# Layer-norm row factors spread through DRAM by DMA instead of by matmul, with weight-set loads moved to ScalarE's queue

## What is computed

```python
h = einsum('bct,bcd->bdt', x, cond_w[subjects])
q, k, v, g = h @ Wq, h @ Wk, h @ Wv, silu(h @ Wg)
beta = sigmoid(h @ Wb + bb)
q = layernorm(silu(causal_dwconv(q, qconv_w, qconv_b)).reshape(Bs, Ls, H, DK), qn_w, qn_b)
k = layernorm(silu(causal_dwconv(k, kconv_w, kconv_b)).reshape(Bs, Ls, H, DK), kn_w, kn_b)
# layernorm: (x - m) * rsqrt(var + eps) * w + b over the 128 of a head
S = (1 - b) * S + b * v[..., :, None] * k[..., None, :];  o = einsum('bhvk,bhk->bhv', S, q)
x = x + (o * g) @ Wo
hd = x @ W.T + ((x @ A.T) @ B.T) * s
x = x + ternary_ffn(hd)          # rms norm, rows quantised to int8, weights -1, 0, 1
```

## Time and profile before

| what | value |
|---|---|
| median of 3 runs | 2684.84 us |
| profiled execution | 2685.08 us |
| its span, first to last instruction | 2683.5 us |
| TensorE busy, matmuls | 95% |
| VectorE, ScalarE, GpSimd busy | 63%, 45%, 26% |
| mean granted clock of TensorE | 0.986 of 2.4 GHz |
| DMA queue of SyncE | 413.63 MB, 48.6% of the 16 engines' span |

### The profile page before, as it was taken

One profiled execution on the slowest core, in us unless ns is written; L12 is line 12 of the kernel. 1 busy time (PEld: TensorE's weight loads), 2 busy tenths in 40 slices (PEclk: granted clock), 3 DMA queues, 4 the chain that ended last, 5 costly groups with the idle time before them and its releaser, 6 DMA issues.

```text
span 2683.5 us, 39968 instructions
## 1 busy us (share of the span) xinstructions
PE 2556.3 (95%) x14536; PEld 1985.0 (74%) x14536; DVE 1688.5 (63%) x2848; ACT 1197.7 (45%) x1878; POOL 696.3 (26%) x764
## 2 busy tenths in 40 slices
PE   5889999999999999999999999999999999999996
PEld 4667777777777777777777777777777777777774
DVE  3766666666666666666656666666666666666653
ACT  3555544544444444354444444353444544444431
POOL 3465522212222212222212222222212212222220
PEclk8999999999999999999999999999999999999998
DMA  6775745445444555355354454444544445444540
GB/s 167 249 224 185 240 154 159 139 155 177 121 142 147 165 166 157 109 172 194 113 173 132 144 177 154 151 139 138 163 148 156 140 149 179 120 146 142 171 132 16
DMA packets 264554, 416.17 MB, mean 155 GB/s; under 512 B 102058, under 2 KB 126634, under 8 KB 264362
## 3 DMA queue, kind: packets, MB, share of 16 engines
q1 hardware_dynamic: 264362, 413.63, 48.6%
HBM read 360.86 MB, written 52.69 MB: 154 GB/s over the span
## 4 chain that ended last, share of the span: by engine, by line
PE 88%; DVE 4%; ACT 3%; issue 2%; SPq 1%; POOL 1%; DMA 0%; ACTq 0%; DVEq 0%; POOLq 0%
PE ring L1048 31%; PE pj_a L1048 26%; PE pj_b L1048 13%; PE ring L1264 4%; PE m L1254 3%; PE var L1222 2%; PE cen_q L1243 2%; PE cen_k L1243 1%; PE cen_k L1244 1%; PE cen_q L1244 1%; PE ring L1149 1%; PE ring L1066 1%; ACT hb L912 1%; PE var L1233 1%; PE m L1264 1%
## 5 line engine op out<-in xcount | busy, mean ns | idle before, releaser
L780 DVE SCALAR_TENSOR_TENSOR y_q<-pj_a,conv,y_q 128x504 f32<-128x504 f32 (+2 forms) x384 | 281.7, 734 | 360.2 <-ACT y_q L963 351.0
L498 POOL TENSOR_TENSOR og_lo<-gt,og_hi 128x512 fp32r<-128x512 f32 x128 | 165.1, 1290 | 922.3 <-ACT og_hi L993 922.3
L1048 PE MATMUL pj_a<-ht_hi,wg 128*128 128x512 f32 x1024 | 352.9, 405 | 2.2 <-DVE y_q L780 2.1
L1048 PE MATMUL pj_a<-ht_hi,wq 128*128 128x512 f32 x1024 | 345.0, 398 | 2.5 <-DVE ht_lo L626 1.5
L1048 PE MATMUL pj_b<-ht_hi,wk 128*128 128x512 f32 x1024 | 335.9, 389 | 0.0
L1048 PE MATMUL ring<-wo,og_hi 128*128 128x512 f32 x1024 | 321.5, 395 | 14.8 <-DVE acc L660 11.8
L1048 PE MATMUL ring<-wv,ht_hi 128*128 128x512 f32 x1024 | 320.8, 394 | 6.8 <-ACT hb L914 6.8
L780 DVE SCALAR_TENSOR_TENSOR y_k<-pj_b,conv,y_k 128x504 f32<-128x504 f32 (+2 forms) x384 | 281.8, 734 | 62.3 <-ACT y_k L963 53.2
L951 ACT ACTIVATE sq_q<-cen_q 128x512 f32<-128x512 f32 x128 | 76.7, 599 | 435.7 <-PE cen_q L1244 435.7
L1048 PEld LDWEIGHTS ring<-wo,og_hi 128*128 128x128 f32 x1024 | 190.4, 189 | 74.2 <-DVE acc L660 18.5
L1048 PEld LDWEIGHTS ring<-wv,ht_hi 128*128 128x128 f32 x1024 | 189.2, 188 | 74.0 <-issue 26.8
(11 more groups left out here) (202 smaller groups left out, 5084.4 us busy)
## 6 DMA issues: line engine op xcount, KB each, us to landing
wq<-parts_q SPq DMA_DIRECT2D x112, 512.0 KB, 4.1
wk<-parts_k SPq DMA_DIRECT2D x112, 512.0 KB, 4.5
wg<-parts_g SPq DMA_DIRECT2D x112, 512.0 KB, 3.7
wv<-parts_v SPq DMA_DIRECT2D x112, 512.0 KB, 6.4
wo<-parts_o SPq DMA_DIRECT2D x112, 512.0 KB, 6.1
keep<-keep_rows SPq DMA_DIRECT2D x256, 64.0 KB, 3.9
wo<-parts_w SPq DMA_DIRECT2D x28, 512.0 KB, 5.6
acc<-in_x_dram SPq DMA_DIRECT2D x8, 1024.0 KB, 5.5
```

The source lines that it names most:

```text
L498: G.tensor_tensor(og_lo[:, u % OG_RING, :], gt[:, u % GT_RING, :], og_hi[:, u % OG_RING, :].bitcast(F32), ALU.subtract).then_inc(S["oglo"], 1)
L780: V.scalar_tensor_tensor(out=yy[:, :, k:], in0=pp[:, :, :L - k], scalar=conv[:, i, h, 3 - k:4 - k], in1=yy[:, :, k:], op0=ALU.mult, op1=AL ...
L1048: last = T.matmul(psum, a, b, start=start and n == 0 and m == 0, stop=stop and n == len(pairs) - 1 and m == 2)
```

## The change

- `spread`, `rstd_hi`, `split_rstd`, the matrix `pick` and what made it are gone. SyncE writes the four rows of `rstd` (partitions 0, 32, 64, 96; 8 KB) to `r_rows` in DRAM, waits for that, and loads each row with a broadcast to all 128 partitions (256 KB each) into the buffers of `sq_q` and `sq_k`, whose squares are used up. `normalise` reads these.
- So `squares` waits for the product of the unit two before, and `seed` waits until the rows of the pair before were written out.
- `variance` stands between the projections of q and k, `seed` before the first tap of k, `newton` between the taps of q and k.
- The loads of whole sets and of x are issued by ScalarE at the start of a slot. The first o quarter of a group is loaded in slot 9 (was 8), the second in 11 (was 10), x in 13 (was 12).
- The first o quarter is made in slot 10 in place of 9, the third set of v from slot 9 in place of 10. The ring of gated heads has 7 places in place of 6.

```diff
-    9: ([("o", 0, 0, 0), ("f", -1, None, 0), ("quant", -1, None, 2), ("quant", -1, None, 3), ("o", 0, 0, 1)],
-        [("o", 0, 0, 2), ("f", -1, None, 1), ("o", 0, 0, 3)]),
-    10: ([("v", 0, 2, 0), ("xqt", -1, None, 2)], [("v", 0, 2, 1), ("xqt", -1, None, 3)]),
+    9: ([("v", 0, 2, 0), ("f", -1, None, 0), ("quant", -1, None, 2), ("quant", -1, None, 3)],
+        [("v", 0, 2, 1), ("f", -1, None, 1)]),
+    10: ([("o", 0, 0, 0), ("xqt", -1, None, 2), ("o", 0, 0, 1)], [("o", 0, 0, 2), ("xqt", -1, None, 3), ("o", 0, 0, 3)]),
...
+            def load_rstd(m):
+                sp.wait_ge(S["rr"], m + 1)
+                for j in range(4 if m else 0):
+                    sp.wait_ge(S[f"r_in_{'qk'[j % 2]}{j // 2}"], 16 * m)
+                sp.dma_start(r_rows, rstd[0:P:32, :]).then_inc(S["r_out"], 16)
+                sp.wait_ge(S["r_out"], 16 * (m + 1))
+                for j in range(4):
+                    x_ = "qk"[j % 2]
+                    sp.dma_start(sq[x_][:, j // 2, :], r_rows[j:j + 1, :].broadcast_to([P, GROUP])).then_inc(S[f"r_in_{x_}{j // 2}"], 16)
...
+                if U % 2 == 0 and 2 <= U <= UNITS:
+                    load_rstd(U // 2 - 1)
                 if H <= U + 1 < UNITS:
                     load_head("g", U + 1)
...
             def normalise(u):
                 for x_ in "qk":
-                    dve.wait_ge(S[f"bc_{x_}"], u + 1)
+                    dve.wait_ge(S[f"r_in_{x_}{u % 2}"], 16 * (u // 2 + 1))
                     dve.wait_ge(S[f"cc_{x_}"], u + 1)
                     c = c_[x_][:, u % C_RING, :]
-                    V.tensor_tensor(c, c, bc_banks[u % 2][x_][:], ALU.mult).then_inc(S[f"n_{x_}"], 1)
+                    V.tensor_tensor(c, c, sq[x_][:, u % 2, :], ALU.mult).then_inc(S[f"n_{x_}"], 1)
...
             def squares(x_, u):
                 act.wait_ge(S[f"cen_{x_}"], u + 1)
                 if u > 1:
-                    act.wait_ge(S["var"], u // 2)
+                    act.wait_ge(S[f"n_{x_}"], u - 1)
...
                 if m:
-                    act.wait_ge(S["r_split"], m)
+                    act.wait_ge(S["r_out"], 16 * m)
...
+            def load_sets(U):
+
+                g, h = divmod(U, H)
+                for part in range(SET):
+                    if g < GROUPS and h in (0, 4, 8, 12) and g * SETS + h // 4 >= SETS:
+                        load_v(g * SETS + h // 4, part)
+                    if h == (1 if g == GROUPS else 2) and g > 1:
+                        load_o(g * SETS - 1, part)
+                    if h == 5 and 1 <= g < GROUPS:
+                        load_w2(g - 1, part)
+                    if h == 9 and 1 <= g < GROUPS:
+                        load_o(g * SETS, part)
+                    if h in (11, 14) and 1 <= g < GROUPS:
+                        load_o(g * SETS + (1 if h == 11 else 2), part)
...
             for U in range(SLOTS):
                 if U < UNITS:
                     project("q", U)
-                    project("k", U)
                 if U % 2 == 0 and 2 <= U <= UNITS:
                     variance(U // 2 - 1)
-                if U % 2 and 0 <= U - 2 < UNITS:
-                    spread(U - 2)
+                if U < UNITS:
+                    project("k", U)
```

More of the change, by code:

```diff
@@ L135, in adaln_attn_ffn @@
         rstd = sb("rstd", [P, GROUP])
-        r_parts = sb("r_parts", [P, GROUP], F32R)
         keep = sb("keep", [P, 2, HALF])
@@ L447, in _ @@
                     sp.dma_start(bias_b, ffn_b.rearrange("(o d) -> o d", o=1).broadcast_to([P, D])).then_inc(S["rows_in"], 16)
-                if h == 8 and 1 <= g < GROUPS:
-                    for part in range(SET):
-                        load_o(g * SETS, part)
+                if U % 2 == 0 and 2 <= U <= UNITS:
+                    load_rstd(U // 2 - 1)
                 if H <= U + 1 < UNITS:
@@ L560, in _ @@
                     step(V.tensor_copy(ident_in[half, t, :], ident[half, half]))
-            step(V.tensor_tensor(signs[:], by32[:, :, 1:2], by32[:, :, 0:1], ALU.subtract))
-            step(V.tensor_reduce(is_low[:], by32[:, :, 1], AX.X, ALU.add))
-            step(V.tensor_scalar(ones, ident[:], 0.0, 1.0, ALU.mult, ALU.add))
-            for j in range(4):
-                step(V.tensor_scalar(pick[:, j, :], ones, signs[:, j, :], 0.0, ALU.mult, ALU.add))
             dve.wait_ge(S["wb_in"], 16)
@@ L831, in _ @@
                     taps("q", U)
+                if U % 2 == 0 and 2 <= U <= UNITS:
+                    newton(U // 2 - 1)
+                if U < UNITS:
                     taps("k", U)
@@ L837, in _ @@
                 take(U, 0)
-                if U % 2 == 0 and 2 <= U <= UNITS:
-                    newton(U // 2 - 1)
                 if 0 <= U - 3 < UNITS:
@@ L843, in _ @@
                     silu_lo("k", U)
-                if U % 2 == 0 and 2 <= U <= UNITS:
-                    split_rstd(U // 2 - 1)
                 take(U, 1)
@@ new lines, in load_o, with load_last_w2 @@
+            def load_o(s, part):
+                if part == 0:
+                    if s % SETS:
+                        act.wait_ge(*made("o", s - 1, HT - 1))
+                    else:
+                        act.wait_ge(*made("h", s // SETS - 1, HT - 1))
+                n = (s % SETS) * SET + part
+                act.dma_start(block_both("o", n), parts["o"][n]).then_inc(S["wo_in"], 16)
+            def load_last_w2(part):
+                if part == 0:
+                    act.wait_ge(*made("v", GROUPS * SETS - 1, HT - 1))
+                act.dma_start(block_both("v", part), parts_w2[part]).then_inc(S["wv_in"], 16)
@@ new lines, in load_w2 @@
+            def load_w2(g, part):
+                if part == 0:
+                    act.wait_ge(*made("o", SETS * g + SETS - 1, HT - 1))
+                    if g == 0:
+                        act.wait_ge(S["saved_o"], 16 * H)
+                        act.wait_ge(S["w2_out"], 64)
+                act.dma_start(block_both("o", part), parts_w2[part]).then_inc(S["wo_in"], 16)
+            def load_sets(U):
[11 more added lines that the diff above has]
+                        load_o(g * SETS + (1 if h == 11 else 2), part)
+                    if U == UNITS:
+                        load_last_w2(part)
+                if h == 13 and g + 1 < GROUPS:
+                    load_x(g + 1)
@@ L1011, in _ @@
                     gated_hi(U - 4)
+                if U % 2 == 0 and 2 <= U <= UNITS:
+                    seed(U // 2 - 1)
                 if U < UNITS:
@@ L1018, in _ @@
                     silu("q", U)
-                if U % 2 == 0 and 2 <= U <= UNITS:
-                    seed(U // 2 - 1)
                 take(U, 0)
```

107 lines of the change are left out of this document (22 added, 85 removed).

## The result

| | before | after |
|---|---|---|
| median of five runs each, us | 2684.84 | 2698.37 (2693.86 to 2701.81) |
| ratio, 95% interval | | 1.0048 [1.0034, 1.0063]: 0.5% slower |
| profiled execution, its span, us | 2685.1, 2683.5 | 2693.9, 2692.1 |
| first group (slots 0 to 15), us | 307.3 | 342.3 |
| groups 1 to 6, mean, us | 322.8 | 318.6 |

What follows compares the result with a forecast made beforehand. TensorE, 95% of the span, was taken as the bound: 2685.1 - 58.4 (`spread` matmuls) - 23.3 (`r_parts` wait) + 8 (exchanged tiles) + 7 (x) + 21 (first group) = 2639.4, stated as 2640 us; range 2606 to 2676.

Steps and rivals of the forecast that it cites:

- The matmuls' price: TensorE: removing the 256 `spread` matmuls, 0.228 us of the stream each, saves 58.4 us.
- The wait for `r_parts`: TensorE's wait before `spread`, 23.3 us in 11 places, was taken to go whole.
- C: Rival, 8%: issues on ScalarE cost twice SyncE's, so TensorE waits before variance in slots 2 and 14; 2660 us.
- D: Rival, 13%: the factors' DRAM round trip misses its slack in every even slot of later groups; 2696 us.
- the estimate of 4.6 us: Factors' write and broadcasts by DMA, reckoned from a skill page as 2.0 + 2.0 + 0.6 us.
- B: Rival, 24%: everything hidden, first-group transfers land as unloaded ones and x costs nothing; 2616 us.
- 7 us for x: Slot 13: x waits for output rows sent in slot 12, costing 1 us per group, 7 us in all.
- quarter and set change places: Slot 10: the third tile waits for its bank 2.3 us, the last 0.4; +1.1 us per group, 8 us.
- the same chain in the first group: First group: row factors stand behind SyncE's saves, costing 3 us in each of 7 slots, 21 us.
- 12.4 against 8.7: hidden: Later groups: factors land at most 8.7 us after the write's issue, allowed 12.4, so the round trip costs nothing.
- The step that lets a set's issues fit in ScalarE's idle time: Slot starts: four issues take 2.52 us, ScalarE idles 3.83 us before its first square; cost nothing.
- the last pair's chain costs nothing: Kernel's end: four o tiles, 11 us, lie beside the last factors' chain; cost 0, bounds 0 and 3 us.

Runs made afterwards that it cites:

- e10: Kernel before, factors still by matmul, but variance, seed, Newton and `r_parts` in their new, earlier places from group 1 on: 2672.3 us, 0.9951.
- e1: Changed kernel with slots 9 and 10 of the first group alone given back their old tiles: 2681.8 us, 0.9986.
- e2: Changed kernel with the old tile table, gated-head ring and places of the output sets in all groups: 2681.9 us, 0.9987.
- e9: e2 plus the edits of e5 and e7, and first-group row factors issued ahead of the raw block of g: 2655.1 us, 0.9880.
- e11: e7 plus e5's moves of VectorE's row products, tiles still exchanged in later groups: 2686.2 us, 1.0002.
- e3: e2 with the row factors of units 0 to 17 spread by matmul as before, DMA from unit 18 on: 2655.7 us, 0.9899.
- e7: e1 with the eight conditioning loads for group 1 issued in twos in slots 5, 7, 9 and 11: 2677.7 us, 0.9974.
- e5: e3 with later groups' row product ahead of the row scales in slot 8 and behind the first take in slot 9: 2629.5 us, 0.9788.
- e6: e3 with only the slot 8 move, VectorE's row product ahead of the row scales in later groups: 2653.5 us, 0.9876.
- e4: Kernel before with only the loads of x and the weight sets, except each group's first o quarter, issued by ScalarE: 2686.5 us, 1.0001.
- e12: e5 with the weight sets and x loaded from SyncE's queue again: 2652.4 us, 0.9874.

## Why the prediction was wrong

**Right.** The matmuls' price: TensorE is busy 7.8 us less in a later group, forecast 7.3. The wait for `r_parts` is gone from slot 8 of later groups and can be saved whole (e10). Four issues cost ScalarE what they cost SyncE (C fell). The chain's 7.2 us stay under its deadline of 12.4 (D fell as a mechanism), though the estimate of 4.6 us, from a section on DMAs that GpSimd issues, was too short, and B, for which it spoke, fell with a first group of 342.3 us. Slot 10's bank wait: 2.05 and 0.54, forecast 2.3 and 0.4. Of the 7 us for x some 1 was paid: ScalarE stands for the output rows in slot 13 and its squares come 3.3 to 4.2 us into it, but in four of seven later groups the slot takes 16.6, the 17.1 of before less two matmuls of 0.23.

**Wrong, "quarter and set change places".** This step reckoned one later group and multiplied. In the first group weights are split in fixed slots that the same table must suit, and the term that was missing is 16.6 us (e1). Without it the change would have come out level with before (0.9986), still far from 2640. In later groups the +1.1 us a group was not tested alone: undoing the exchange there changed nothing while VectorE's order stayed (e1 and e2), and 31 us with it mended (e9 and e11).

**Mis-sized, "the same chain in the first group".** The mechanism was right: the write behind saves, product, squares and raw blocks late, slots 5, 7, 11 and 13 longer. I took 21 us with a ceiling of 35. Measured, the way by DMA costs the first 18 units 26 us net (e2 to e3); e3 also carries 36 `spread` matmuls (8 us) and 9 us of waits for `r_parts`, so the gross price is some 43. Three us for each slot left out the eight conditioning issues (4 us, e7, 9 in the profiled execution) and the half clock. The 4.5 us taken for a write behind saves is the row of loads of wk, not of saves; the writes themselves took 2.0 to 4.7 us there.

**Wrong, "12.4 against 8.7: hidden".** I tested the new wait of the squares against the landing and in slot 66, where VectorE is free. It binds at the start of slot 9, on the product of slot 8, where the transfer has landed and VectorE comes late to the product. With the tiles in their old places slot 9 is 3.6 us longer than before (e2), and mending VectorE's order brings back 3.4 us a group, 26 us by the medians (e5 against e3). How much of it is the squares' wait itself is open: e6 removed that wait and gained 2 us, and e5 also moves a product that stood ahead of the accumulation before the change. In the kernel as changed the squares start 3.1 us into slot 9 as in e2, and TensorE waits 0.42 and 1.74 there; that this comes from the same lateness was argued from the order, and e11 shows that the same edit doesn't mend it. The step that lets a set's issues fit in ScalarE's idle time failed for slot 9 as well: the squares start 0.5 us into it without the load (e5) and 3.0 with it (e11).

**Wrong, "the last pair's chain costs nothing".** From the last group's start to the end the time fell by 0.65 us where some 7 were forecast. This wait of TensorE was 0.89 there:

```profile
2616.11 1.12 PE L1227 MATMUL m<-c_q,c_k 128*64 128x64 f32 x16 [3.91 <-POOL c_k L456]
```

Four o tiles lie beside the chain, but scores and attention behind them don't. The wait is 3.9 in e3 and e5 too, and 0.9 in e4 and e10, which have no factors by DMA; an attention wait of 1.31 behind it goes, so it costs 1.7 net. TensorE's wait before the last variance, 1.67 for 0.75, is in e4 as well and so comes from the loads that ScalarE issues. The largest part is clock: stretches at 1.2 GHz add up to 38.8 us there for 29.7, some 4.5 us of time by half of the difference. What brought that on is open.

**Weighed and left out of the sum.** The Trainium skill, "DMA: Bandwidth & Descriptors", "Issuing engines are not separate DMA queues", says that a second issuing engine saves only issue time. e4 agrees, 1.0001. In e12 issue time and the order on the queue, with the clock that followed, were worth 23 us.

## What to carry to other kernels

A change to a table that a whole program shares is reckoned in its odd stretch too: here the first group, where the same slots also prepare weights. When a buffer gets a second use, list who now waits for its reader, and look at that wait in the slot where the reader's engine is fullest, not in the emptiest one. Here the round trip to DRAM was hidden where SyncE's queue had room; in the first group, where that queue was full, it and all behind it paid, and moving it only named another payer. Loads moved to a working engine's queue stand ahead of that engine's own work: find the slot in which it has no idle time.

## What the hardware showed

A wait on TensorE has a second price. With the 4.0 us of e2 came 3.4 us at 1.2 GHz in each later group, beginning within some 0.5 us of the wait's end, and a matmul took 0.63 us in them for 0.39. With waits of some 2.0 us in the same place they came in one group of seven in e5 and in five of seven in e12. So the wait can be read from a plan, but in these runs the clock could not be foretold from the wait.

Steps of VectorE on 128x2 numbers took up to 1.22 us for 0.16 while GpSimd worked on 128x512 (e6). The two steps ended at 836.16 and 837.42 and GpSimd's two additions at 836.15 and 837.40, so each step ended with an addition. e5 shows the same.
